# B's projection and split moved to the first stage, and one product with C per batch given to GpSimd

## The chip, the cores and the metric

One Trainium2 chip, one core, one launch. The metric is device time in microseconds. An execution of the kernel before takes 2493.12 us (median of three, 2491.65 to 2495.48). The engines are named as in the profile: PE is TensorE (PEld its weight loads), DVE is VectorE, ACT is ScalarE, POOL is GpSimd, SP is SyncE, which here only issues DMAs.

## What is computed

For 32 batches x of 512 rows and 256 columns, fp32: a layer norm without scale gives xn, and the output is the sum of x, a selective state-space scan and a mixture of experts that choose their rows.

```python
x, xn = x, layernorm(x)
# the scan, per batch: 256 channels d, 16 states s, 512 times l
deltaBC = xn @ W_deltaBC.T                    # 64 + 16 + 16 columns
delta, B, C = split(deltaBC, [64, 80])
delta = softplus(delta @ W_dt.T + b_dt)
h[l] = exp(delta[l] * A[s]) * h[l-1] + delta[l] * B[l, s] * xn[l]
y = sum_s h[l] * C[l, s] + D * xn
# the experts: 8 of them, each takes the 128 rows of a batch it likes best
S = softmax(xn @ Wg.T); G, I = top_k(S.T, 128)
out[I] += G * (gelu(xn[I] @ W1 + b1) @ W2 + b2)
return x + y + out
```

## The kernel before

Partitions hold channels in the scan (256 channels are two halves, so a tile of one batch is 128 partitions x 1024 columns, times along the columns) and rows elsewhere. The program is written out by hand, engine by engine, with semaphores; every engine runs its queue in order. There are three stretches.

**First stage** (`rows`, lines 285, 411, 539, 775 and 925; 32 iterations, software pipelined). SP loads x of batch b (line 293) into a ring of four and stores the normalized rows of batch b-3 to HBM (line 297). VectorE takes the statistics (801, 819, 828, 814), GpSimd the power and the last quarter of the normalization (417, 424), ScalarE the other three quarters (557). TensorE transposes xn (938), ScalarE copies the transposed tile to SBUF (567), and TensorE forms the router's logits (951) with weights widened so that four batches fill the 32 rows of one bank. Once per four batches VectorE copies these logits to SBUF (`lgt`, line 788), TensorE turns them to rows (960), and VectorE and ScalarE do the softmax. The load of batch b waits until batch b-4 is normalized.

**Top-k** (`top_round`, line 743): rounds of max, index, replace on VectorE for two halves of the batches. GpSimd gathers the chosen rows (`gather`, 447 to 449) once the first half's picks are out (855); TensorE transposes them (`chosen_columns`, 980).

**Main stage** (`main`, one iteration per batch and four slots `sl` of four steps each; step n of 16 is one state s). Per step:

- TensorE spreads row n of B over 128 partitions (`spread_b`, 1008), from `bcs`, which holds B as three bf16 parts whose sum is the fp32 value; it waits for the previous product with B, since there is one bank.
- VectorE runs the scan (896) over two banks `bank_x` that alternate, in place; then the product du x B of the next step (`multiply_b`, 842); then the product with C into one of four `prod` buffers (905).
- ScalarE makes the decays exp(delta A) (629), one slot ahead.
- GpSimd adds the product to `ysum` (494).

Between these, TensorE and ScalarE run the expert's two matrix products for a unit of 256 rows per slot (1102, 1121, 638, 688), GpSimd issues two gathers at the slot's first step (449) and two accumulating scatters at the second and third (513), and once per batch the accumulating store of y (526), which waits for y's own copies and, where a scatter to the same batch has just gone out, for its landing.

The next batch but one is prepared within a batch. `project` (966 to 972, at slot 0) computes the 96 rows of deltaBC; ScalarE copies them (`take_bc`, 580) and rounds them to bf16 (582); GpSimd subtracts (`take_rest`, 436, at slot 1); ScalarE rounds the rest (`take_mid`, 595); GpSimd subtracts again (`take_lo`, 442, at slot 2, after its step 9). SP moves C to HBM and the three parts of B to `bcs` (`move_high`, `move_mid`, `move_low`, 331 to 344), and loads C back, broadcast over the partitions, one slot ahead (`load_c`, 351). `expand` (977) multiplies by W_dt, ScalarE takes softplus (604 to 613), and GpSimd makes delta (457) and du = delta x xn (463) at slot 3, after its sum of step 12. `multiply_b` for step 0 of the next batch, issued by VectorE at step 15, waits for that du:

```python
dve.wait_ge(b_ready, s + 1)
dve.wait_ge(du_done, b + 1)
wait(dve, prod_done, s - 1)
```

Of the kernel before, what the change touches and what calls it, by code (L numbers as in the profile page):

```python
# [35 lines left out]
P = 128  # L36
# [4 lines left out]
BC = R + 2 * N  # L41
HALF = NB // 2
# [4 lines left out]
BODY = 4  # L47
BU = BODY * SLOTS
# [22 lines left out]
def build(nc, x, wdbc, wdt, bdt, alog, dpar, wg, w1, b1, w2, b2, out):  # L71
    ctx = ExitStack()
    with ctx:  # L73
# [10 lines left out]
        c_rows = nc.dram_tensor("c_rows", [NB, N, T], F32, kind="Internal").ap()  # L84
# [13 lines left out]
        wdbc_sb = sb("wdbc_sb", [P, HC, BC])  # L98
# [4 lines left out]
        wg_sb = sb("wg_sb", [P, HC, E])  # L103
# [14 lines left out]
        zabs = sb("zabs", [P, HC, T])  # L118
        yrow = sb("yrow", [P, TC, D])
        bc_all = sb("bc_all", [BC, T])  # L120
        bc_hi = sb("bc_hi", [P, T], BF16)
        bc_mid = sb("bc_mid", [P, T], BF16)
        bc_lo = sb("bc_lo", [P, T], BF16)
        bc_rest = sb("bc_rest", [P, T])
# [28 lines left out]
        wg_wide = small(HC * GATE, GATE * E)  # L153
        lgt = small(1, T)[0:GATE * E, 0]
        work = prod[:, 0, :, :]
        vals, idx_f = small(2, K), small(2, K)
# [22 lines left out]
        wide_set = sem("wide_set")  # L179
# [18 lines left out]
        lgt_done = sem("lgt_done")  # L198
# [17 lines left out]
        bc_proj = sem("bc_proj")  # L216
        hi_done = sem("hi_done")
        all_done = sem("all_done")
# [3 lines left out]
        hi_moved = sem("hi_moved")  # L222
        lo_moved = sem("lo_moved")
        mid_moved = sem("mid_moved")
# [8 lines left out]
        c_out = sem("c_out")  # L233
# [3 lines left out]
        prod_done = sem("prod_done")  # L237
        sum_done = sem("sum_done")
# [15 lines left out]
        def batch_of(u, i):  # L254

            return u // 64 * HALF + u % 8 * UB + i

# [13 lines left out]
        def _(sp):  # L271
# [12 lines left out]

            def rows(q):
                for r in range(ROWS):
# [22 lines left out]
            load_w2(0, 0, 0)  # L309

# [17 lines left out]
            def move_high(nb, par, used):  # L328

                held(all_done, nb)  # L330
                sp.dma_start(c_rows[nb - 1], bc_all[BC - N:BC, :]).then_inc(c_out, 16)
                held(hi_done, nb)
                held(b_ready, used)
                sp.dma_start(bcs[0:32, par], bc_hi[64:96, :]).then_inc(hi_moved, 16)

            def move_mid(nb, par):

                held(mid_done, nb)
                sp.dma_start(bcs[32:64, par], bc_mid[64:96, :]).then_inc(mid_moved, 16)

            def move_low(nb, par):

                held(lo_done, nb)
                sp.dma_start(bcs[64:96, par], bc_lo[64:96, :]).then_inc(lo_moved, 16)

            def load_c(u):

                held(c_out, (u // SLOTS + 1) * 16)
                held(prod_done, (u - 1) * STEPS)
                first = u % SLOTS * STEPS  # L350
                sp.dma_start(c_all[:, u % 2], c_rows[u // SLOTS:u // SLOTS + 1, first:first + STEPS, :]
                             .broadcast_to([P, STEPS, T])).then_inc(c_in[u % 2], 16)
# [44 lines left out]
        def _(pool):  # L397
# [33 lines left out]
            def take_rest(nb):  # L431

                pool.wait_ge(all_done, nb)
                pool.wait_ge(hi_done, nb)
                wait(pool, lo_done, nb - 1)
                nc.gpsimd.tensor_tensor(bc_rest[0:BC, :], bc_all[:], bc_hi[0:BC, :], ALU.subtract).then_inc(rest_done, 1)  # L436

            def take_lo(nb):

                pool.wait_ge(mid_done, nb)  # L440
                wait(pool, lo_moved, nb * 16 - 16)
                nc.gpsimd.tensor_tensor(bc_lo[0:BC, :], bc_rest[0:BC, :], bc_mid[0:BC, :], ALU.subtract).then_inc(lo_done, 1)

# [30 lines left out]
            def main(j):  # L474
                for k in range(BU):
# [56 lines left out]
        def _(act):  # L532
            for dst, src in ((wg_sb[:], wg.rearrange("(c p) e -> p c e", p=P)), (a_sb[:], alog), (b2_f, b2),
                             (wdbc_sb[:], wdbc.rearrange("(c p) m -> p c m", p=P)), (wdt_sb[:], wdt),
# [4 lines left out]
            def rows(q):  # L539
                for r in range(ROWS):  # L540
# [19 lines left out]
                    if there(b - 2, NB):  # L560
# [6 lines left out]
                        nc.scalar.copy(xtr[:, par], tr_banks[par]).then_inc(xnt_done, 2)  # L567
                    if r % GATE == 1 and there(g - 2, NB // GATE):
# [5 lines left out]
            def take_bc(nb):  # L574

                act.wait_ge(bc_proj, nb)
                wait(act, rest_done, nb - 1)
                wait(act, z_done, nb * 2 - 2)
                wait(act, c_out, nb * 16 - 16)
                nc.scalar.copy(bc_all[:], bank_t[0:BC, :]).then_inc(all_done, 1)  # L580
                wait(act, hi_moved, nb * 16 - 16)
                nc.scalar.copy(bc_hi[0:BC, :], bank_t[0:BC, :]).then_inc(hi_done, 1)  # L582
# [6 lines left out]

            def take_mid(nb):  # L590

                act.wait_ge(rest_done, nb)
                wait(act, mid_moved, nb * 16 - 16)
                wait(act, lo_done, nb - 1)
                nc.scalar.copy(bc_mid[0:BC, :], bc_rest[0:BC, :]).then_inc(mid_done, 1)

# [44 lines left out]
            def take_xr(b, par, dt):  # L641

                act.wait_ge(xr_tr, (b - 2) * HC + dt + 1)
                if dt == 0:
                    act.wait_ge(du_done, b - 1)
                    act.wait_ge(skip_done, b - 1)
                    act.wait_ge(bc_proj, b - 1)
# [15 lines left out]
            take_bc(1)  # L663
            take_mid(1)
# [5 lines left out]
            decays(0, 0, 0, 0, 1, range(STEPS))  # L670
            act.wait_ge(b1_in, 16)
# [3 lines left out]
            def main(j):  # L675
                for k in range(BU):
# [34 lines left out]
                    if there(b, NB) and there(b + 1, NB):  # L711
                        if sl == 2:
                            softplus_ln(b + 2)
                        if sl == 0:
                            take_bc(b + 2)
                        if sl == 1:
                            take_mid(b + 2)
# [455 lines left out]
```

## Time and profile before

| | |
|---|---|
| median of three runs | 2493.12 us |
| the profiled execution | 2495.35 us |
| its span | 2493.5 us |
| granted TensorE clock, mean | 0.982 |
| DMA | 325.4 MB, mean 130 GB/s |

The span is one execution from its first to its last instruction; the profiled execution's own time is 1.85 us longer. Busy times are sums over an engine's instructions, with overlaps counted once. A row of instructions reads: line, engine, operation, output<-input, shape, count | busy us, mean ns of one | idle time of the engine before them and what ended it. TensorE runs four passes over fp32 data, in two instructions. GpSimd's recorded durations include time spent behind an instruction that has not ended, so that start-to-start distances say more than means.

### The profile page before, as it was taken

The page shows a single profiled execution, that of the slowest core. Times are in us where ns is not written, and L with a number is a line of the kernel's source. Part 1 is how long each engine was busy: PE and PEld are TensorE (multiplying, and loading weights), DVE is VectorE, ACT ScalarE, POOL GpSimd, SP SyncE. Part 2 cuts the span into 40 slices and gives each one's busy share as a digit, 9 for nine tenths or more (in the row PEclk, how much of TensorE's full clock was granted, in tenths as well). Part 3 has the DMA queues.
Part 4 walks back from the last instruction along what each step waited for, and adds up shares of the span by engine and source line. Part 5 has one row for each costly group of instructions (what it writes and reads, how often), then busy time and mean ns, then how long its engine had stood idle before and what let it go on. Part 6 is the DMA issues. An engine that isn't in the chain of part 4 may idle for free. (4 is left out here: it accounts for less than half of the span.)

```text
span 2493.5 us, 32910 instructions
## 1 busy us (share of the span) xinstructions
PE 2356.9 (95%) x10524; PEld 1773.7 (71%) x10524; DVE 2417.3 (97%) x2090; ACT 1971.3 (79%) x3432; POOL 2200.3 (88%) x1260
## 2 busy tenths in 40 slices
PE   7828999999999999999999999999999999999996
PEld 3306777777777777777777777777777777777775
DVE  6599999999999999999999999999999999999995
ACT  6627888888888888888888888888888888888783
POOL 4316999999999999999999999999999999999996
PEclk9958999999999999999999999999999999999998
DMA  9872455444445453454535344444444445453443
GB/s 303 274 270 69 136 167 140 117 124 112 135 117 137 102 137 108 117 132 98 154 99 146 95 133 107 127 123 117 133 116 125 108 115 133 100 150 93 106 91 53
DMA packets 162973, 325.38 MB, mean 130 GB/s; under 512 B 16272, under 2 KB 133104, under 8 KB 146160
## 3 DMA queue, kind: packets, MB, share of 16 engines
q1 hardware_dynamic: 95536, 239.11, 28.0%
q0 software_dynamic: 66048, 83.92, 20.1%
q8 instruction: 85, 1.39, 0.2%
q14 instruction: 88, 0.72, 0.1%
q10 hardware_dynamic: 1216, 0.23, 0.0%
HBM read 250.84 MB, written 84.93 MB: 135 GB/s over the span
## 5 line engine op out<-in xcount | busy, mean ns | idle before, releaser
L494 POOL TENSOR_TENSOR ysum<-ysum,prod 128x1024 f32<-128x1024 f32 x480 | 1307.1, 2723 | 33.4 <-DVE prod L905 24.4
L896 DVE TENSOR_TENSOR_SCAN bank_x<-decay,bank_x 128x1024 f32<-128x1024 f32 x512 | 1167.2, 2280 | 0.0
L1102 PE MATMUL bank_l<-ext,w_sb 128*128 128x256 f32 x4096 | 970.3, 382 | 0.8 <-ACT og L688 0.8
L1121 PE MATMUL bank_l<-w_sb,hid 128*128 128x256 f32 x4096 | 957.2, 383 | 0.0
L1121 PEld LDWEIGHTS bank_l<-w_sb,hid 128*128 128x128 f32 x4096 | 762.6, 190 | 163.4 <-issue 67.7
L1102 PEld LDWEIGHTS bank_l<-ext,w_sb 128*128 128x128 f32 x4096 | 756.5, 190 | 136.2 <-issue 23.5
L638 ACT ACTIVATE hid<-bank_l,b_all 128x256 f32<-128x256 f32 x1024 | 430.9, 475 | 332.6 <-PE bank_l L1102 329.4
L629 ACT ACTIVATE decay<-delta,a_sb 128x511 f32<-128x511 f32 x1024 | 640.0, 708 | 1.2
L905 DVE TENSOR_TENSOR prod<-bank_x,c_all 128x1024 f32<-128x1024 f32 x512 | 620.4, 1212 | 0.1
L842 DVE TENSOR_TENSOR bank_x<-du,bank_b 128x1024 f32<-128x1024 f32 x512 | 613.4, 1198 | 0.0
L513 POOL DMA_INDIRECT out<-og,idx_all x256 | 408.6, 1596 | 49.5 <-POOL ysum L494 35.4
L449 POOL DMA_INDIRECT ex<-xn_rows,idx_all x256 | 258.0, 1008 | 85.2 <-issue 47.0
L1008 PE MATMUL bank_b<-bcs,pick 96*128 96x512 bf16 x512 | 197.4, 386 | 35.4 <-DVE bank_x L842 28.8
L1008 PEld LDWEIGHTS bank_b<-bcs,pick 96*128 96x128 bf16 x512 | 49.5, 97 | 147.3 <-DVE bank_x L842 118.6
L629 ACT ACT_TABLE_LOAD x98 | 125.7, 1283 | 4.2 <-POOL delta L457 2.5
L722 ACT ACT_TABLE_LOAD x95 | 121.9, 1283 | 1.7
L688 ACT ACTIVATE og<-bank_l,gate_all 128x256 f32<-128x256 f32 x256 | 105.0, 460 | 11.3 <-PE bank_l L1121 11.3
L494 POOL TENSOR_TENSOR ysum<-skip,prod 128x1024 f32<-128x1024 f32 x32 | 91.8, 2868 | 11.1 <-DVE prod L905 11.1
L654 ACT COPY ext<-bank_t 128x512 f32<-128x512 f32 x128 | 76.0, 594 | 28.0 <-PE bank_t L986 28.0
L417 POOL TENSOR_TENSOR hid<-hid,neg_half 128x4 f32<-128x4 f32 x32 | 32.3, 1008 | 68.0 <-DVE hid L828 65.9
L436 POOL TENSOR_TENSOR bc_rest<-bc_all,bc_hi 96x512 f32<-96x512 f32 x32 | 68.7, 2146 | 19.9 <-ACT bc_hi L582 19.9
L986 PE MATMUL bank_t<-ident,ex 128*128 128x128 f32 x512 | 77.3, 274 | 6.6 <-DMA ex<-xn_rows,idx_all 6.6
(95 smaller groups left out, 1577.9 us busy)
## 6 DMA issues: line engine op xcount, KB each, us to landing
c_all<-c_rows SPq DMA_DIRECT2D x128, 1024.0 KB, 5.4
w_sb<-in_w SPq DMA_DIRECT2D x32, 1024.0 KB, 6.2
decay<-in_x SPq DMA_DIRECT2D x32, 512.0 KB, 5.4
xn_rows<-decay SPq DMA_DIRECT2D x32, 512.0 KB, 4.0
out<-yrow POOLq DMA_DIRECT2D x32, 512.0 KB
xr<-xn_rows SPq DMA_DIRECT2D x30, 512.0 KB, 6.5
ex<-xn_rows,idx_all POOLq DMA_INDIRECT x256
out<-og,idx_all POOLq DMA_INDIRECT x256, 4.1
```

The source lines that it names most:

```text
L449: pool.indirect_dma_start(out=ex[:, u % 2, i], out_offset=None, in_=xn_rows, in_offset=bass.IndirectOffsetOnAxis(ap=idx_all[:, u * UB + i: ...
L494: nc.gpsimd.tensor_tensor(ysum[:, m % 2], first, prod[:, i], ALU.add).then_inc(sum_done, 1)
L513: pool.indirect_dma_start(out=out_rows, out_offset=bass.IndirectOffsetOnAxis(ap=idx_all[:, w * UB + c:w * UB + c + 1], axis=0), in_=og[:, ...
L629: nc.scalar.activation(decay[:, par, i, dt, 1:T], delta[:, dpar_, dt, 1:T], ACT.Exp, scale=a_sb[:, dt, n:n + 1]).then_inc(decay_done, 1)
L638: nc.scalar.activation(hid[:, k % 2, f], bank_l[(pair + k) % 2][:, (f % 2) * UT:(f % 2 + 1) * UT], ACT.Gelu_apprx_tanh, bias=b1_all[:, exp ...
L722: nc.scalar.activation(warm[:], bdt_sb[:, 0:1], ACT.Gelu_apprx_tanh)
L842: nc.vector.tensor_tensor(bank_x[:, s % 2].rearrange("p (c t) -> p c t", c=HC), du[:, par], bank_b[:][:, None, :].broadcast_to([P, HC, T]) ...
L896: nc.vector.tensor_tensor_scan(bank_x[:, s % 2], decay[:, k % 2, i].rearrange("p c t -> p (c t)"), bank_x[:, s % 2], 0.0, ALU.mult, ALU.ad ...
L905: nc.vector.tensor_tensor(prod[:, i], bank_x[:, s % 2].rearrange("p (c t) -> p c t", c=HC), c_all[:, u % 2, i][:, None, :].broadcast_to([P ...
L1008: nc.tensor.matmul(bank_b[:], pick[:, n:n + 1].broadcast_to([3 * 2 * N, P]), bcs[:, par], start=True, stop=True).then_inc(b_ready, 1)
L1102: i = nc.tensor.matmul(bank_l[(q + k) % 2][:, (f % 2) * UT:(f % 2 + 1) * UT], w1_sb[:, e2, hc, f * P:(f + 1) * P], ext[:, k % 2, hc], star ...
L1121: i = nc.tensor.matmul(o, hid[:, (k - 1) % 2, f, c * K:(c + 1) * K], w2_sb[:, le2, f], start=False, stop=(f == FC - 1 and c == UB - 1))
```

## The change

B and C are projected in the first stage: the router's weights and those of deltaBC stand side by side (`wpj_sb`, 8 + 96 columns), each batch's 104 rows are copied by ScalarE into a ring of four (`proj`), and SP stores 96 of them to HBM (`bc_rows`) and the 16 rows of B to SBUF, eight batches to a tile of 128 partitions (`b_whole`). The split of B into three bf16 parts is then done on four such tiles, between the first stage and the main stage, and stored to HBM (`b_rows`). In the main stage SP loads the 64 rows for `expand` (`load_rank`, slot 0) and the three parts of B (`load_b`, slot 1) per batch. `project`, `take_bc`, `take_rest`, `take_mid`, `take_lo` and the `move_` functions are gone; so are the widened weights and VectorE's copy of the logits.

Step n = 4 of each batch: the scan writes to a tile in SBUF (`state`), VectorE leaves out the product with C, and GpSimd does it, ahead of its sum.

```diff
+PJ = E + BC
+SPLIT = P // N
+NG = NB // SPLIT
+GP_STEP = 4
...
+        def gp_prods(s):
+
+            return (s + N - 1 - GP_STEP) // N
+
+        def dve_prods(s):
+
+            return s - gp_prods(s)
...
+            def store_proj(b):
+
+                held(proj_done, b + 1)
+                sp.dma_start(bc_rows[b], proj[E:PJ, b % 4]).then_inc(proj_out[b % 4], 16)
+                sp.dma_start(b_whole[b % SPLIT * N:b % SPLIT * N + N, b // SPLIT],
+                             proj[E + R:E + R + N, b % 4]).then_inc(proj_out[b % 4], 16)
+
+            def store_parts(g):
+
+                for part, done in enumerate((hi_done, mid_done, lo_done)):
+                    held(done, g + 1)
+                    sp.dma_start(b_rows[part, g * P:(g + 1) * P, :], b_parts[:, part, g % 2]).then_inc(parts_out[g % 2], 16)
+
+            def load_b(nb, par, used):
+
+                g = (nb - 1) // SPLIT
+                held(parts_out[g % 2], (g // 2 + 1) * 48)
+                held(b_ready, used)
+                held(stack_set, 1)
+                for part in range(3):
+                    sp.dma_start(bcs[2 * N * part:2 * N * part + N, par],
+                                 b_rows[part, nb * N - N:nb * N, :]).then_inc(b_in[par], 16)
+
+            def load_rank(nb):
+
+                held(z_done, nb * 2 - 2)
+                sp.dma_start(rank[:], bc_rows[nb - 1, 0:R, :]).then_inc(rank_in, 16)
...
+                    if there(b - 6, NB):
+                        store_proj(b - 6)
...
             load_w2(0, 0, 0)
+            for r in range(4):
+                held(proj_out[r], 32 * NB // 4)
+            load_rank(1)
+            store_parts(0)
+            load_b(1, 0, 0)
...
-            move_high(1, 0, 0)
-            move_mid(1, 0)
-            move_low(1, 0)
             load_c(0)
+            for g in range(1, NG):
+                store_parts(g)
             for part in range(4, HALF // UB):
                 residual(part)
...
+                    if sl == 0 and there(b + 1, NB):
+                        load_rank(b + 2)
                     if sl == 1 and there(b + 1, NB):
-                        move_high(b + 2, (m + 1) % 2, b * N)
-                    if sl == 2 and there(b + 1, NB):
-                        move_mid(b + 2, (m + 1) % 2)
-                    if sl == 3 and there(b + 1, NB):
-                        move_low(b + 2, (m + 1) % 2)
+                        load_b(b + 2, (m + 1) % 2, b * N)
...
         @block.gpsimd
-            take_rest(1)
-            take_lo(1)
+            split_rest(0)
+            split_lo(0)
             take_delta(1, 0)
             take_du(1, 0, 16)
+            for g in range(1, NG):
+                split_rest(g)
+                split_lo(g)
...
-                            pool.wait_ge(prod_done, s + 1)
+                            if n == GP_STEP:
+                                pool.wait_ge(scan_done, s + 1)
+                                pool.wait_ge(c_in[u % 2], (u // 2 + 1) * 16)
+                                wait(pool, sum_done, s - 3)
+                                nc.gpsimd.tensor_tensor(prod[:, i], state[:], c_all[:, u % 2, i][:, None, :].broadcast_to([P, HC, T]),
+                                                        ALU.mult).then_inc(gp_prod_done, 1)
+                                pool.wait_ge(gp_prod_done, b + 1)
+                            else:
+                                pool.wait_ge(prod_done, dve_prods(s + 1))
...
-                        if sl == 1 and i == 0 and there(b, NB) and there(b + 1, NB):
-                            take_rest(b + 2)
-                        if sl == 2 and i == 1 and there(b, NB) and there(b + 1, NB):
-                            take_lo(b + 2)
...
         @block.scalar
+                    if there(b - 3, NB):
+                        act.wait_ge(logits_done, b - 2)
+                        wait(act, proj_out[(r - 3) % 4], (b - 3) // 4 * 32)
+                        wait(act, lg_tr, (b - 3) // GATE)
+                        nc.scalar.copy(proj[:, (r - 3) % 4], lg_banks[(r - 3) % 2][0:PJ, :]).then_inc(proj_done, 1)
...
             skip_term(0, 16, 0)
-            take_bc(1)
-            take_mid(1)
+            split_hi(0)
+            split_mid(0)
...
             decays(0, 0, 0, 0, 1, range(STEPS))
+            for g in range(1, NG):
+                split_hi(g)
+                split_mid(g)
...
         @block.vector
-                    if r % GATE == 3 and there(g - 1, NB // GATE):
-
-                        dve.wait_ge(logits_done, g * GATE)
-                        wait(dve, lg_tr, g - 1)
-                        nc.vector.tensor_copy(lgt, lg_banks[gp][0:GATE * E, :]).then_inc(lgt_done, 1)
...
-                wait(dve, prod_done, s - 1)
+                if (s - 2) % N == GP_STEP:
+                    wait(dve, scan_done, s - 1)
+                else:
+                    wait(dve, prod_done, dve_prods(s - 1))
...
-                        nc.vector.tensor_tensor_scan(bank_x[:, s % 2], decay[:, k % 2, i].rearrange("p c t -> p (c t)"),
+                        if n == GP_STEP:
+                            wait(dve, gp_prod_done, b)
+                            into = state[:].rearrange("p c t -> p (c t)")
+                        else:
+                            into = bank_x[:, s % 2]
+                        nc.vector.tensor_tensor_scan(into, decay[:, k % 2, i].rearrange("p c t -> p (c t)"),
                                                      bank_x[:, s % 2], 0.0, ALU.mult, ALU.add).then_inc(scan_done, 1)
...
+                        if n == GP_STEP:
+                            continue
...
         @block.tensor
                         for hc in range(HC):
-                            i = nc.tensor.matmul(lg[0:GATE * E, :], wg_wide[:, hc * GATE + place], xtr[:, pp, hc],
-                                                 start=(place == 0 and hc == 0), stop=(place == GATE - 1 and hc == HC - 1))
+                            i = nc.tensor.matmul(lg_banks[pp][0:PJ, :], wpj_sb[:, hc], xtr[:, pp, hc],
+                                                 start=(hc == 0), stop=(hc == HC - 1))
...
-                        pe.wait_ge(lgt_done, g)
+                        pe.wait_ge(proj_done, g * GATE)
                         wait(pe, lsh_done, g - 1)
                         for c in range(TC):
-                            i = nc.tensor.transpose(bank_t[:, c * GATE * E:(c + 1) * GATE * E], lgt[:, c * P:(c + 1) * P],
-                                                    ident[0:GATE * E, 0:GATE * E])
+                            for place in range(GATE):
+                                i = nc.tensor.transpose(bank_t[:, (c * GATE + place) * E:(c * GATE + place + 1) * E],
+                                                        proj[0:E, place, c * P:(c + 1) * P], ident[0:E, 0:E])
...
-                pe.wait_ge(all_done, nb)
-                nc.tensor.matmul(bank_t[:], wdt_sb[:, dt * P:(dt + 1) * P], bc_all[0:R, :],
+                pe.wait_ge(rank_in, nb * 16)
+                nc.tensor.matmul(bank_t[:], wdt_sb[:, dt * P:(dt + 1) * P], rank[:],
```

## Rows read from the trace of the kernel before

**Rows 1.** The page, part 1: busy us of each engine, share of the span, instructions.

```profile
PE 2356.9 (95%) x10524; PEld 1773.7 (71%) x10524; DVE 2417.3 (97%) x2090; ACT 1971.3 (79%) x3432; POOL 2200.3 (88%) x1260
```

**Rows 2.** Busy us by stretch: PE, PEld, DVE, ACT, POOL, then granted clock, DMA share, GB/s.

```profile
50.00:70.00 20.00, 17.97 (x78) 7.60 (x76) 13.91 (x71) 14.36 (x26) 8.48 (x13) 1.00 0.99 328
...
90.00:122.00 32.00, 26.48 (x106) 11.49 (x107) 17.69 (x87) 20.31 (x36) 11.79 (x16) 0.89 0.67 218
...
192.00:2480.00 2288.00, 2245.31 (x10085) 1725.52 (x10084) 2273.30 (x1538) 1870.42 (x3268) 2134.02 (x1174) 1.00 0.46 119
```

**Rows 3.** Timeline of VectorE from 1112 us: start, duration, engine, line.

```profile
1112.16 2.28 DVE L896 TENSOR_TENSOR_SCAN bank_x<-decay,bank_x 128x1024 f32<-128x1024 f32 x1
1114.35 1.20 DVE L842 TENSOR_TENSOR bank_x<-du,bank_b 128x1024 f32<-128x1024 f32 x1
1115.47 1.21 DVE L905 TENSOR_TENSOR prod<-bank_x,c_all 128x1024 f32<-128x1024 f32 x1
1116.60 2.28 DVE L896 TENSOR_TENSOR_SCAN bank_x<-decay,bank_x 128x1024 f32<-128x1024 f32 x1
```

**Rows 4.** Line 494, 780 to 1350 us: durations min/median/max ns, first and last start.

```profile
L494 POOL TENSOR_TENSOR ysum<-skip,prod x8: 2867/2878/2887, 840.7 to 1336.6; 128x1024 f32<-128x1024 f32 x8
```

**Rows 5.** Groups of GpSimd: the sums, 780 to 1350 us, then the whole span.

```profile
L494 POOL TENSOR_TENSOR ysum<-ysum,prod 128x1024 f32<-128x1024 f32 x122 | 334.4, 2741 | 2.8
...
L494 POOL TENSOR_TENSOR ysum<-ysum,prod 128x1024 f32<-128x1024 f32 x480 | 1307.1, 2723 | 33.4 <-DVE prod L905 24.4
```

**Rows 6.** Timeline of GpSimd: in the top-k, then from 1106 and from 1147 us.

```profile
140.63 1.15 POOL L436 TENSOR_TENSOR bc_rest<-bc_all,bc_hi 96x512 f32<-96x512 f32 x1 [19.90 <-ACT bc_hi L582]
...
1106.60 2.35 POOL L457 TENSOR_TENSOR delta<-delta,zabs 128x1024 f32<-128x1024 f32 x1
1109.08 2.37 POOL L463 TENSOR_TENSOR du<-delta,xnt 128x1024 f32<-128x1024 f32 x1
...
1147.46 2.38 POOL L494 TENSOR_TENSOR ysum<-ysum,prod 128x1024 f32<-128x1024 f32 x1
1150.01 1.64 POOL L513 DMA_INDIRECT out<-og,idx_all  x1 [0.17 <-POOL ysum L494]
...
1163.14 2.38 POOL L494 TENSOR_TENSOR ysum<-ysum,prod 128x1024 f32<-128x1024 f32 x1
...
1166.80 1.62 POOL L513 DMA_INDIRECT out<-og,idx_all  x1 [0.17 <-issue]
```

**Rows 7.** Timeline of GpSimd at 715 us, batch 7: the store of y.

```profile
715.09 1.39 POOL L526 DMA_DIRECT2D out<-yrow  x1 [2.05 <-DMA out<-og,idx_all]
```

**Rows 8.** Who waited for whom, 780 to 1350 us: total us, times, longest.

```profile
PEld bank_b L1008 <- DVE bank_x L842: 28.2, 63, 0.6
```

**Rows 9.** Groups of VectorE, ScalarE and TensorE, 0 to 137 us.

```profile
L801 DVE BATCH_NORM_STATS2 hid<-decay 128x6 f32<-128x256 f32 x128 | 44.7, 409 | 26.8 <-DMA decay<-in_x 26.8
...
L788 DVE COPY hid<-bank_x 32x512 f32<-32x512 f32 x8 | 5.4, 679 | 16.1 <-PE bank_x L951 16.1
...
L557 ACT ACTIVATE decay<-decay,hid 128x256 f32<-128x256 f32 x96 | 50.6, 591 | 31.1 <-DVE hid L814 31.0
...
L960 PE MATMUL bank_t<-ident,hid 32*128 32x32 f32 x32 | 3.4, 227 | 0.8 <-DVE hid L788 0.8
```

**Rows 10.** DMA queues, 0 to 115 us: packets, MB, share of 16 engines.

```profile
q1 hardware_dynamic: 33019, 34.34, 90.5%
```

**Rows 11.** Timeline of the hand-over, 154 to 192 us, and DMA issues 125 to 192 us.

```profile
154.26 5.00 ACT L629 ACTIVATE decay<-delta,a_sb 128x511 f32<-128x511 f32 x8
...
181.61 1.24 POOL L449 DMA_INDIRECT ex<-xn_rows,idx_all  x1 [26.30 <-DVE gate_all L855]
...
186.03 1.09 PE L986 MATMUL bank_t<-ident,ex 128*128 128x128 f32 x4 [6.64 <-DMA ex<-xn_rows,idx_all]
...
191.76 0.47 PE L1033 MATMUL bank_l<-ident,hid 128*128 128x128 f32 x1 [4.64 <-DVE hid L848]
...
out<-in_x SPq DMA_DIRECT2D x10, 11.8
```

More of the change, by code:

```diff
@@ L118, in build @@
         zabs = sb("zabs", [P, HC, T])
+        state = sb("state", [P, HC, T])
         yrow = sb("yrow", [P, TC, D])
[L120 to L124, printed above, removed]
+        rank = sb("rank", [R, T])
+        b_parts = sb("b_parts", [P, 3, 2, T], BF16)
         bcs = sb("bcs", [3 * 2 * N, 2, T], BF16)
@@ L152, in build @@
         lmax, lsum, lrec = (small(2, TC * GATE) for _ in range(3))
-        wg_wide = small(HC * GATE, GATE * E)
-        lgt = small(1, T)[0:GATE * E, 0]
         work = prod[:, 0, :, :]
+        proj = prod[0:PJ, 2:4, :, :].rearrange("p a b t -> p (a b) t")
+        b_whole = ysum[:, :, :, :].rearrange("p a b t -> p (a b) t")
         vals, idx_f = small(2, K), small(2, K)
@@ L197, in build @@
         logits_done = sem("logits_done")
-        lgt_done = sem("lgt_done")
+        proj_done = sem("proj_done")
+        proj_out = [sem(f"proj_out{i}") for i in range(4)]
         lg_tr = sem("lg_tr")
@@ L221, in build @@
         lo_done = sem("lo_done")
-        hi_moved = sem("hi_moved")
-        lo_moved = sem("lo_moved")
-        mid_moved = sem("mid_moved")
+        parts_out = [sem(f"parts_out{i}") for i in range(2)]
+        rank_in = sem("rank_in")
+        b_in = [sem(f"b_in{i}") for i in range(2)]
         z_done = sem("z_done")
@@ L326, in _ @@
                 residual(part)
[L328 to L344, printed above, removed]
             def load_c(u):
-                held(c_out, (u // SLOTS + 1) * 16)
-                held(prod_done, (u - 1) * STEPS)
+                held(prod_done, dve_prods((u - 1) * STEPS))
+                held(gp_prod_done, gp_prods((u - 1) * STEPS))
                 first = u % SLOTS * STEPS
-                sp.dma_start(c_all[:, u % 2], c_rows[u // SLOTS:u // SLOTS + 1, first:first + STEPS, :]
+                sp.dma_start(c_all[:, u % 2], bc_rows[u // SLOTS:u // SLOTS + 1, R + N + first:R + N + first + STEPS, :]
                              .broadcast_to([P, STEPS, T])).then_inc(c_in[u % 2], 16)
-            move_high(1, 0, 0)
-            move_mid(1, 0)
-            move_low(1, 0)
             load_c(0)
+            for g in range(1, NG):
+                store_parts(g)
             for part in range(4, HALF // UB):
@@ L429, in _, with split_rest, split_lo @@
                 pool.wait_ge(rows_out[r], 16 * NB // 4)
[L431 to L442, printed above, removed]
+            def split_rest(g):
+                pool.wait_ge(hi_done, g + 1)
+                nc.gpsimd.tensor_tensor(b_whole[:, g], b_whole[:, g], b_parts[:, 0, g % 2], ALU.subtract).then_inc(rest_done, 1)
+            def split_lo(g):
+                pool.wait_ge(mid_done, g + 1)
+                wait(pool, parts_out[g % 2], g // 2 * 48)
+                nc.gpsimd.tensor_tensor(b_parts[:, 2, g % 2], b_whole[:, g], b_parts[:, 1, g % 2], ALU.subtract).then_inc(lo_done, 1)
             def gather(u):
@@ L572, in _, with split_hi, split_mid @@
             through(rows, NB // ROWS)
[L574 to L582, printed above, removed]
+            def split_hi(g):
+                for r in range(4):
+                    act.wait_ge(proj_out[r], (g + 1) * SPLIT // 4 * 32)
+                wait(act, parts_out[g % 2], g // 2 * 48)
+                nc.scalar.copy(b_parts[:, 0, g % 2], b_whole[:, g]).then_inc(hi_done, 1)
+            def split_mid(g):
+                act.wait_ge(rest_done, g + 1)
+                wait(act, parts_out[g % 2], g // 2 * 48)
+                nc.scalar.copy(b_parts[:, 1, g % 2], b_whole[:, g]).then_inc(mid_done, 1)
             def take_yrow(half, taken, added):
@@ L588, in take_yrow @@
                 nc.scalar.copy(yrow[:, 2 * half:2 * half + 2], bank_t[:].rearrange("p (c d) -> p c d", c=2)).then_inc(yrow_done, 1)
[L590 to L595, printed above, removed]
             def take_z(nb, par, dt):
@@ L768, in parameters @@
                 nc.vector.tensor_copy(b2_lo, b2_f).then_inc(b2_step, 1)
-                for hc in range(HC):
-                    for place in range(GATE):
-                        dve.wait_ge(wide_set, 1)
-                        nc.vector.tensor_copy(wg_wide[:, hc * GATE + place, place * E:(place + 1) * E], wg_sb[:, hc]).then_inc(wide_set, 1)
             def rows(q):
@@ L1009, in spread_b, with stack_whole @@
                                  start=True, stop=True).then_inc(b_ready, 1)
-            def stack_whole(b):
-                pe.wait_ge(hi_moved, b * 16 + 16)
-                pe.wait_ge(mid_moved, b * 16 + 16)
-                pe.wait_ge(lo_moved, b * 16 + 16)
+            def stack_whole(par, count):
+                pe.wait_ge(b_in[par], count)
             pe.wait_ge(pick_made, 4)
@@ L1036, in _ @@
             picks_lines(0)
-            stack_whole(0)
+            stack_whole(0, 48)
             spread_b(0, 0, 0)
@@ L1072, in main @@
                                 pe.wait_ge(xnt_in[m % 2], (b // 2 + 1) * 16 + (sl + 1) * 16 // HC)
-                            if sl == 1 and there(b + 1, NB):
-                                pe.wait_ge(all_done, b + 2)
-                                pe.wait_ge(hi_done, b + 2)
                             if sl == 2 and there(b + 1, NB):
```

45 lines of the change are left out of this document (12 added, 33 removed).

## The prediction

> **What bounds it now.** I read the busy totals first, then the stages, then a step of VectorE, then GpSimd. VectorE is busy 2417 us and GpSimd 2200, TensorE 2357 [rows 1]. By stage [rows 2], the first stage (layernorm, router, rows written) runs to about 122 us with the DMA engines at a share of 0.99 until 90 and 0.67 after that; the top-k rounds fill the time to 192; the main stage lasts 2288 us, of which VectorE works 2273. There one step is scan, next product with B, product with C, starting at 1112.16, 1114.35, 1115.47, and the next scan at 1116.60 [rows 3]: 2.19 + 1.12 + 1.13 = 4.44 us, so 71.04 us for a batch of sixteen. VectorE never pauses.
>
> GpSimd is the one to look at twice. Its share, 88%, suggests room. But eight starts of its first sum of a batch lie between 840.7 and 1336.6 us, seven intervals of **70.84 us**, 0.20 less than VectorE's 71.04 [rows 4]. In the same stretch its 122 other sums waited 2.8 us in all [rows 5]. What the page counts as idle there is gaps between instructions, not waiting. Its lag shrinks by 0.2 us per batch and that is all the slack it has; over the whole run its sums waited 24.4 us for VectorE's product [rows 5], most of it in the first two and the last batch, where its DMAs are fewer.
>
> Where does GpSimd hold VectorE? Not at the sums: four buffers of products let it lag three steps, 13 us. At du: the product with B for step 0 of the next batch is issued behind the scan of step 15 and waits for du, which GpSimd makes only after sum 12. Du starts at 1109.08 and takes 2.37, so it is there at 1111.45; the product starts at 1114.35 [rows 3, 6]. Slack: **2.9 us**.
>
> **The change, part by part.**
>
> VectorE in the main stage: one product with C per batch goes. The step keeps 2.19, and the next scan now directly follows the product with B whose output it needs, so that one shows its full 1.20 and not 1.12, with a few hundredths for the semaphore. 4.44 becomes about 3.43: 1.0 us per batch, 32 us in all, if nothing else holds it. The scan that writes to SBUF I take at the old 2.19: it reads the same operands, one in SBUF and one in PSUM. Bounds: it may be a few hundredths shorter or longer, 32 x 0.1 = 3 us each way.
>
> GpSimd in the main stage: bc_rest and bc_lo go, the multiply comes. Rest takes 1.15 us where nothing overlaps it, at 140.63 [rows 6]; the 2.1 us mean of the page counts time behind an earlier instruction. Lo: from the sum at 1163.14 to the scatter at 1166.80 is 3.66, the same pair without lo is 1147.46 to 1150.01, 2.55, so 1.11. Removed: 2.26. The multiply has the shape of delta and du (128x1024 f32): delta to du, start to start, is 2.48 [rows 6], and the sum behind the multiply waits for it like du for delta. Added: 2.3 to 2.5; I take 2.45. Net +0.19, so GpSimd's own batch is 70.84 + 0.19 = 71.03 us, against a VectorE that could do 70.0. **The product leaves one full engine for another full one.** From the third or fourth batch on VectorE, 2.9 us ahead, stalls about 1 us per batch at the product with B for step 0, and the period stays 71.0.
>
> Bounds of the multiply: at 2.3 the net is +0.04, 29 batches give 4 us less; at the mean that the page's rows give for a sum, 2.72 [rows 5], plus 0.15 for the dependence, +0.6, 12 us more. I take 2.45 because the nearest row is du's. GPSIMD Engine Reference of the Trainium skill, section 3.1, gives 4497 ns for an fp32 tensor_tensor of 2048 columns, half of which is 2.25 us here, an estimate; by it the main stage would come out 6 us shorter than by the 2.45 taken.
>
> What GpSimd's timeline gives: in the first two batches it waits for VectorE, and so wins about 1.5 us there from the shorter step. At batch 7, and by the same condition at 23, it waits 2.05 us at the output DMA of y for its own scatter to land [rows 7]; 0.2 of that is an ordinary gap. Before, VectorE did not feel it (the lag ate it); now GpSimd sets the pace and both count: 2 x 1.85 = 3.7. Twenty-nine batches at 71.03 for 71.04: -0.3. GpSimd at the last du: +1.9. VectorE may be 2.9 ahead of where it stood: -1.0; its last batch has no du behind it and gives its own -1.0. **Main stage: -2 us**, from -9 to +12.
>
> TensorE: the projection leaves the main stage (4 passes of 512 columns, under 2 us per batch) and sixteen spreads of B stay. Its weight load waited 28.2 us for VectorE's product with B in 128 steps [rows 8], 0.22 per step; so it has 3.5 us per batch before and about 5 after. One short step of 3.4 us leaves it behind by less than 1 us, and the spread is early by more. Nothing. ScalarE loses three copies per batch; it waits for TensorE anyway: nothing. SP's queue in the main stage: four small moves go, four come (rank, three of B) ahead of load_rows; the loads of C keep their place. Nothing: they are needed several steps later.
>
> First stage. The matmul has 104 output rows for 32, same columns: no cost. ScalarE gets a copy of about 0.6 us per batch; it idled 31.1 us for VectorE's shift over 32 batches [rows 9], so most is covered. Sixteen transposes of 8 rows per group for four: 3.4 us of TensorE for 32 now [rows 9], about 10 us for 128, spread over 32 batches, covered except once at the end (+1.3 us). VectorE's copy of the logits goes and with it 16.1 us of in-order waiting for TensorE [rows 9], which delayed the statistics behind it.
>
> The DMAs are what counts. Each batch stores 96 rows of 2 KB to HBM and 16 rows to SBUF: 229 KB beside 1049 KB. The engines moved 34.3 MB in 33019 packets with 90.5% of their time [rows 10] (115 us): 50 ns per 1 KB packet, and 328 GB/s at share 0.99 [rows 2]. So a batch was 3.2 us and the stores add 0.70. Twenty-six batches are stored before the last load. Those of the first 90 us, some 21, cost in full, for the engines are full there: 15 us. The others fall where a third of DMA time is idle [rows 2], and there VectorE's waits for the logits go too: I give back 6. **First stage: +9, with its end +10**, from +2 (the stores fill gaps, the stall was the limit) to +24 (0.70 plus some of SP's two further issues, on each of 26 batches, and nothing given back).
>
> The hand-over. VectorE's top-k follows the first stage without a gap, so the chain of batch 0 (skip, split, z, softplus, delta, du, decays) is hidden: its decays ended at 159.3 while VectorE left its rounds at 191.7 [rows 11]. It starts ahead by no projection and now has split 0 in it; same length. But SP is now held in the stores of splits 1 to 3, which ScalarE makes only behind the first decays, some 34 us into the top-k; six residual parts (11.8 us each to landing in their queue [rows 11]) and two weight loads go out behind them and meet the first gather. That one was issued at 181.61 and consumed at 186.03, and the second TensorE step needed by VectorE came at 191.76; 4.6 us of room [rows 11]. I take **+2**, from 0 to +8.
>
> Sum: +10 + 2 - 2 = +10 us. The profiled execution took 2495.35 us, its span 2493.5, so 2505.4; the median of the three runs is 2.2 lower: **2503 us**.
>
> **Rivals.**
>
> *The saving arrives.* GpSimd's own batch falls to 70.0 or the idle 5% of its share is real. VectorE then saves 32 us: 2493 - 32 + 12 = 2473. It decides if the multiply costs under 1.5 us. For it: the share in the totals. Against: [rows 4, 6]. Chance 0.08.
>
> *The first stage hides its stores.* It was bound by the loop load, statistics, normalize, next load, with VectorE's wait for the logits in it. Then +2, hand-over 0 and main -6: 2489. For it: VectorE waited 26.8 us for loads and 16.1 for logits [rows 9], so both limits are near. Against: share 0.99. Chance 0.17.
>
> *Small DMAs cost by the piece.* Two more per batch on one queue, each with an issue of its own; if 0.9 us of issue adds to the 0.70: 26 x 1.6 = +42, 2533. For it: the load is issued behind them. Against: the issues run while the engines still work on the last store. Chance 0.07. DMA: Bandwidth & Descriptors of the Trainium skill, section on measured bandwidth, says that transfers under 64 KB are dominated by descriptors; the 16-row store is 32 KB.
>
> *GpSimd's multiply is dear* (2.9 to 3.0 with its waits): VectorE follows at 71.5, main +12, 2517. Chance 0.10.
>
> **How the numbers follow.** Forecast 0.58 at 2503, its own range 2494 to 2513. A change of 0.2%, 5 us, is about what a measurement can tell. Faster (below 2488): the first rival and part of the second, 0.15. Same (2488 to 2498): the rest of the second and the low side of the forecast, 0.22. Slower: 0.63. For 8 in 10 the range is 2486 to 2518.
>
> **What would show it.** Right: GpSimd's first sums 71.0 us apart; VectorE idle ahead of the product with B about 1 us per batch, released by du; the short step 3.4 us; the multiply 2.3 to 2.5 us; first stage share near 1 to its end, top-k starting about 10 us later. Wrong: VectorE without idle time in the main stage, first sums 70.0 apart, or a first stage that ends at 137 as before.

## The result: 2506.06 us, 0.45% slower

The median of six runs is 2506.06 us (2501.0 to 2509.6), beside 2493.19 for the kernel before (six runs): a ratio over the runs of 1.0045, 95% interval 1.0033 to 1.0056. The medians differ by 12.9 us (a quotient of 1.0052, inside the interval); 2503 was forecast. The profiled execution, the slowest of the six, spans 2507.8 us, 14.3 more than before, and this difference can be placed. The page of the kernel after, part 1, answers to [rows 1]; the stretches (PE, PEld, DVE, ACT, POOL, granted clock, DMA share, GB/s) to [rows 2]:

```profile
PE 2301.7 (92%) x10492; PEld 1770.6 (71%) x10492; DVE 2383.0 (95%) x2042; ACT 1949.0 (78%) x3376; POOL 2217.3 (88%) x1236
```
```profile
50.00:70.00 20.00, 16.27 (x77) 9.44 (x76) 10.72 (x57) 14.78 (x27) 7.76 (x11) 0.91 1.02 328
...
90.00:122.00 32.00, 23.84 (x120) 14.38 (x119) 15.11 (x79) 20.29 (x36) 10.76 (x15) 0.89 0.99 327
...
205.00:2490.00 2285.00, 2185.43 (x9961) 1704.86 (x9961) 2242.74 (x1505) 1830.48 (x3176) 2142.97 (x1143) 1.00 0.46 120
```

VectorE's total fell by 34 us and nothing came of it: in the main stage it is now busy 2243 of 2285 us. The DMA engines, at 0.67 of their time from 90 to 122 us before, are at 0.99 there.

**First stage and hand-over.** VectorE's timeline after; the statistics of the last batch began at 116.45 before, VectorE's first product with B at 191.62, its first scan 1.55 later:

```profile
127.67 1.41 DVE L818 BATCH_NORM_STATS2 hid<-decay 128x6 f32<-128x256 f32 x4 [2.60 <-DMA decay<-in_x]
...
202.71 1.22 DVE L862 TENSOR_TENSOR bank_x<-du,bank_b 128x1024 f32<-128x1024 f32 x1
207.56 0.37 DVE L875 CAST idx_all<-bank_l 128x128 uint32<-128x128 f32 x1 [3.62 <-PE bank_l L1047]
...
208.00 2.27 DVE L921 TENSOR_TENSOR_SCAN bank_x<-decay,bank_x 128x1024 f32<-128x1024 f32 x1
```

The first stage gives +11.1 (202.71 against 191.62) and the hand-over +3.7 (from the product to the scan 5.29 against 1.55 us). In the second, VectorE waited for TensorE, and TensorE for the gathered rows:

```profile
206.01 1.09 PE L1003 MATMUL bank_t<-ident,ex 128*128 128x128 f32 x4 [15.52 <-DMA ex<-xn_rows,idx_all]
```

**Main stage.** From the first scan to the end of the last product, 2271.9 us after (208.00 to 2479.90) and 2272.2 before. VectorE's timeline at a batch's end and at its step 4:

```profile
1122.48 2.29 DVE L921 TENSOR_TENSOR_SCAN bank_x<-decay,bank_x 128x1024 f32<-128x1024 f32 x1
1125.67 1.23 DVE L862 TENSOR_TENSOR bank_x<-du,bank_b 128x1024 f32<-128x1024 f32 x1 [0.90 <-POOL du L484]
...
1145.70 2.28 DVE L921 TENSOR_TENSOR_SCAN state<-decay,bank_x 128x1024 f32<-128x1024 f32 x1
1147.89 1.21 DVE L862 TENSOR_TENSOR bank_x<-du,bank_b 128x1024 f32<-128x1024 f32 x1
1149.23 2.30 DVE L921 TENSOR_TENSOR_SCAN bank_x<-decay,bank_x 128x1024 f32<-128x1024 f32 x1
```

The short step is 3.53 us for 4.44 [rows 3]: 0.91 gained. At the end of the same batch VectorE waits 0.90 for du. Over the run that wait is the largest that VectorE has in the main stage (groups of VectorE, whole span):

```profile
L862 DVE TENSOR_TENSOR bank_x<-du,bank_b 128x1024 f32<-128x1024 f32 x512 | 617.1, 1205 | 24.9 <-POOL du L484 24.9
L921 DVE TENSOR_TENSOR_SCAN state<-decay,bank_x 128x1024 f32<-128x1024 f32 x32 | 72.9, 2277 | 0.0
```

GpSimd, its timeline around the same places and its first sums (800 to 1370 us), which answer to [rows 4, 6]:

```profile
1123.21 2.37 POOL L484 TENSOR_TENSOR du<-delta,xnt 128x1024 f32<-128x1024 f32 x1
...
1153.64 1.95 POOL L554 DMA_DIRECT2D out<-yrow  x1
1154.50 3.51 POOL L514 TENSOR_TENSOR prod<-state,c_all 128x1024 f32<-128x1024 f32 x1
1158.08 2.36 POOL L526 TENSOR_TENSOR ysum<-ysum,prod 128x1024 f32<-128x1024 f32 x1
```
```profile
L526 POOL TENSOR_TENSOR ysum<-skip,prod x8: 2892/2898/2922, 853.5 to 1352.4; 128x1024 f32<-128x1024 f32 x8
```

Seven intervals in 498.9 us: 71.27 us per batch in the mean, where it was 70.84. Six of them are 71.13 to 71.20 us; the seventh, from 1209.25 to 1281.24, is 71.99 and has in it a wait of 0.76 us at the store of y. So GpSimd's ordinary batch is 71.17 us. Du ends at 1125.58 and VectorE's product starts 0.09 later. The page's 3407 ns mean for the multiply counts the tail of the DMA issue ahead of it; from that issue's end, 1155.59, to the multiply's, 1158.01, are 2.42 us.

### The profile page after: what moved, and what is told of

The parts are those of the page before. It is cut to its first block and busy times, and to the rows that moved or that the text cites. A ratio compares the mean times of both kernels' runs of the same rounds, so it can differ in the third digit from the quotient of the medians.

```text
span 2507.8 us, 32574 instructions
## 1 busy us (share of the span) xinstructions
PE 2301.7 (92%) x10492; PEld 1770.6 (71%) x10492; DVE 2383.0 (95%) x2042; ACT 1949.0 (78%) x3376; POOL 2217.3 (88%) x1236
## 5 line engine op out<-in xcount | busy, mean ns | idle before, releaser
L526 POOL TENSOR_TENSOR ysum<-ysum,prod 128x1024 f32<-128x1024 f32 x480 | 1274.3, 2655 | 25.8 <-DVE prod L932 12.5
L921 DVE TENSOR_TENSOR_SCAN bank_x<-decay,bank_x 128x1024 f32<-128x1024 f32 x480 | 1097.5, 2286 | 4.6 <-DVE bank_x L862 0.5
L862 DVE TENSOR_TENSOR bank_x<-du,bank_b 128x1024 f32<-128x1024 f32 x512 | 617.1, 1205 | 24.9 <-POOL du L484 24.9
L932 DVE TENSOR_TENSOR prod<-bank_x,c_all 128x1024 f32<-128x1024 f32 x480 | 584.6, 1218 | 0.1
L749 ACT ACT_TABLE_LOAD x95 | 121.9, 1283 | 1.7
L514 POOL TENSOR_TENSOR prod<-state,c_all 128x1024 f32<-128x1024 f32 x32 | 109.0, 3407 | 0.0
L818 DVE BATCH_NORM_STATS2 hid<-decay 128x6 f32<-128x256 f32 x128 | 44.9, 413 | 55.8 <-DMA decay<-in_x 55.8
```

The costliest lines, as they stand in the source:

```text
L526: nc.gpsimd.tensor_tensor(ysum[:, m % 2], first, prod[:, i], ALU.add).then_inc(sum_done, 1)
L749: nc.scalar.activation(warm[:], bdt_sb[:, 0:1], ACT.Gelu_apprx_tanh)
L862: nc.vector.tensor_tensor(bank_x[:, s % 2].rearrange("p (c t) -> p c t", c=HC), du[:, par], bank_b[:][:, None, :].broadcast_to([P, HC, T]) ...
L921: nc.vector.tensor_tensor_scan(into, decay[:, k % 2, i].rearrange("p c t -> p (c t)"), bank_x[:, s % 2], 0.0, ALU.mult, ALU.add).then_inc( ...
L932: nc.vector.tensor_tensor(prod[:, i], bank_x[:, s % 2].rearrange("p (c t) -> p c t", c=HC), c_all[:, u % 2, i][:, None, :].broadcast_to([P ...
```

## The experiments

Each experiment was timed beside runs of the kernel before, whose median was 2494.34 or 2494.69 us (2493.19 beside the change). Ratios are to those runs; the times are medians, and a difference of two experiments' medians carries about 1.5 us from this.

**e1: the product back to VectorE.**

```diff
         def gp_prods(s):
 
-            return (s + N - 1 - GP_STEP) // N
+            return sum(1 for b in range(NB) if gp_batch(b) and b * N + GP_STEP < s)
+
+        def gp_batch(b):
+
+            return False
...
-                            if n == GP_STEP:
+                            if n == GP_STEP and gp_batch(b):
```

> The changed kernel with the product of step 4 given back to VectorE in every batch; projection and split stay in the first stage. If GpSimd sets the pace of the main stage (its batch 71.17 us, of which the multiply is some 2.5): GpSimd falls to about 68.7 us per batch, VectorE never waits for du and runs at 71.03, and the main stage is as long as with the product on GpSimd: 2506 us, within 3. If instead GpSimd's product does save VectorE its 0.91 us in most batches: 32 x 0.9 = 29 us more, 2535.

2508.74 us, ratio 1.0057 (1.0041 to 1.0072), which overlaps the change's. From the first scan to the end of the last product it takes 2272.3 us, for 2271.9 with the product on GpSimd. VectorE's wait for du is gone and its batch is 71.03 us. Moving a whole product per batch off the engine that was 97% busy was worth nothing in the main stage; so the 12.9 us are not the product's either.

**e2: no multiply.**

```diff
                                 pool.wait_ge(scan_done, s + 1)
-                                pool.wait_ge(c_in[u % 2], (u // 2 + 1) * 16)
-                                wait(pool, sum_done, s - 3)
-                                nc.gpsimd.tensor_tensor(prod[:, i], state[:], c_all[:, u % 2, i][:, None, :].broadcast_to([P, HC, T]),
-                                                        ALU.mult).then_inc(gp_prod_done, 1)
-                                pool.wait_ge(gp_prod_done, b + 1)
```

(and the two waits for `gp_prod_done` on SP and VectorE)

> The changed kernel without GpSimd's multiply (the product of state 4 with C is left out of the output; the sum adds what lies in its buffer, so the sums stay sixteen). If the multiply's time on GpSimd is what VectorE waits for at du: no wait there, batches of 70.12 us, 32 x 0.9 = 29 us less, 2477. If the wait at du has another origin (ScalarE's softplus late, the scatters, TensorE): GpSimd's batch shrinks but the wait stays, 2500 to 2506.

2479.06 us, ratio 0.9941 (0.9926 to 0.9956): 27 us less than the change; its output lacks the product of step 4. From the first scan to the end of the last product it takes 2244.7 us, 27.2 less. The wait for du is gone (groups of VectorE, whole span):

```profile
L856 DVE TENSOR_TENSOR bank_x<-du,bank_b 128x1024 f32<-128x1024 f32 x512 | 616.5, 1204 | 0.6 <-PE bank_b L1018 0.6
```

So the saving of 0.91 us per batch is real and is kept back by the multiply's time on GpSimd, by nothing on ScalarE or TensorE.

**e3: two batches of three.** As e1, with `return b % 3 != 2`.

> The product of step 4 is GpSimd's in two batches of three, VectorE's in the third. If both engines' loads simply add: GpSimd 3 x 71.17 - 2.5 = 211.0 us for three batches, VectorE 3 x 71.03 - 2 x 0.91 = 211.3, so both near 70.4 per batch and the slack of 2.9 us at du carries the difference: 32 x 0.6 = 19 us less, 2487. If GpSimd's bound is not its own load but something that scales with every batch: 2500 or more.

2487.89 us, ratio 0.9972 (0.9962 to 0.9982): faster than the kernel before, with every result computed. The two engines' loads do add as supposed: GpSimd's first sums in eight batches, and VectorE's product with B:

```profile
L530 POOL TENSOR_TENSOR ysum<-skip,prod x8: 2878/2893/2911, 849.5 to 1342.9; 128x1024 f32<-128x1024 f32 x8
```
```profile
L866 DVE TENSOR_TENSOR bank_x<-du,bank_b 128x1024 f32<-128x1024 f32 x512 | 617.7, 1206 | 0.6 <-POOL du L488 0.6
```

70.49 us per batch, and 0.6 us of waiting for du in the whole run. Each engine has a little left in the average; the slack at du carries the two heavy batches.

**e7: the product alone, in the kernel before.** The edits of step 4 and their counts put into the kernel before; projection and split stay where they were.

> The kernel before with GpSimd's product alone; projection and split stay in the main stage. If GpSimd paces: its batch is 70.85 + 0.32 + 2.26 = 73.4 us, 2.4 above VectorE's 71.03, over 30 batches +72, with the waits at y that now show (+3.7) less VectorE's head start of 3 and its last batch: 2565. If GpSimd has the room that its share of 88% suggests: VectorE's saving arrives, 32 x 0.9 = 29 us less, 2464.

2558.16 us, ratio 1.0255 (1.0240 to 1.0271). The first sums lie (1367.1 - 853.5) / 7 = 73.37 us apart, as forecast; VectorE waits for du in nearly every batch:

```profile
L514 POOL TENSOR_TENSOR ysum<-skip,prod x8: 2890/2904/2913, 853.5 to 1367.1; 128x1024 f32<-128x1024 f32 x8
```
```profile
L865 DVE TENSOR_TENSOR bank_x<-du,bank_b 128x1024 f32<-128x1024 f32 x512 | 616.7, 1204 | 88.6 <-POOL du L475 88.6
```

The total was put 7 us too high. Counted from the first scan, GpSimd's last first sum comes 67.6 us later than before, where 72 + 3.7 had been forecast. The waits at the store of y are a part of that: the longer intervals around them (73.58 to 73.81) add some 1.4 us in all for the 3.7. The rest is that about 29 batches, not 30, ran 2.3 us longer, not 2.4. This run also gives both terms of GpSimd's sum by themselves. Six of the seven intervals above are 73.29 to 73.36 us, 73.34 in the mean. So the product costs 73.34 - 70.84 = **2.50 us** per batch, and taking the split out of the main stage gives 73.34 - 71.17 = **2.17**.

**e5 and e6: what the first stage pays for.**

```diff
                 sp.dma_start(bc_rows[b], proj[E:PJ, b % 4]).then_inc(proj_out[b % 4], 16)
+                sp.dma_start(bc_twice[b], proj[E:PJ, b % 4]).then_inc(proj_out[b % 4], 16)
```

> In the changed kernel each batch's 96 projected rows are stored to HBM twice, the second time to a tensor that nobody reads: 197 KB more per batch. If the first stage is bound by bytes on the DMA engines: 0.60 us at 328 GB/s on 26 batches, +16, 2522. If it is bound by the piece (issue and completion of each DMA): 0.9 us or more each, +23 or more, 2530. If it is bound by ScalarE's copies or the loop of load and normalization: under +6, 2506 to 2512.

```diff
-                sp.dma_start(b_whole[b % SPLIT * N:b % SPLIT * N + N, b // SPLIT],
-                             proj[E + R:E + R + N, b % 4]).then_inc(proj_out[b % 4], 16)
...
             load_rank(1)
+            for g in range(NG):
+                sp.dma_start(b_whole[:, g], bc_rows[g * SPLIT:(g + 1) * SPLIT, R:R + N, :]).then_inc(whole_in[g], 16)
             store_parts(0)
```

> The changed kernel without the 16-row store to SBUF per batch: the tiles of B for the split are loaded from HBM in four DMAs after the first stage. One DMA of 32 KB less per batch. By bytes: 0.10 us on 26 batches, -2.6, 2503.5. By the piece: 0.4 us or more each, -10 or more, 2496 or less. If the loads afterwards delay the chain of batch 0 they are hidden behind the top-k.

e5: 2524.57 us, 1.0121 (1.0105 to 1.0136), 18.5 more than the change, where 16 were due by bytes and 23 or more by the piece. Its last batch's statistics start at 141.37 us, 14.8 later than the mean of the kernels with the change's first stage, which is 0.57 us for a store of 197 KB. So bytes bind, and not ScalarE's copies or the load loop.

e6: 2499.53 us, 1.0022 (1.0013 to 1.0031), 6.5 less than the change and between my two figures. In e6's timeline of VectorE the last batch's statistics start at 121.53, where the change's start at 127.67:

```profile
121.53 1.40 DVE L818 BATCH_NORM_STATS2 hid<-decay 128x6 f32<-128x256 f32 x4 [1.95 <-DMA decay<-in_x]
```

One execution of each is not enough here. The six kernels whose first stage is the change's (after, e1 to e4, e9) start these statistics between 123.6 and 128.4 us, 126.6 in the mean; the three without the small store (e6, e8, e10) between 119.7 and 121.9, 121.1 in the mean. That is 5.5 us on 26 batches, or 0.21 for a store of 32 KB whose bytes are worth 0.10. The medians say less. E6's 6.5 us hold a shorter hand-over too: its first scan is 1.56 us behind the product and not 5.29. E8, which has e6's edit and e3's with a hand-over as long as e3's (5.43 and 5.34 us), is 4.2 us faster than e3, or 0.16 per store, with intervals that overlap. DMA: Bandwidth & Descriptors of the Trainium skill, section on measured bandwidth, calls transfers below 64 KB descriptor-dominated. A price above that of the bytes goes that way, but between 0.10 and 0.21 us these runs do not settle it. Why e6's hand-over is short is open: SP's order behind the split is the change's, and in e8, which has the same loads of B, the wait is back.

**e4 and e9: the hand-over.** e4 puts `residual(4..7)` ahead of `store_parts(1..3)`. e9 adds:

```diff
-                    if sl != 0:
+                    if sl != (1 if b == 0 else 0):
                         continue
```

> SP issues the four residual parts before the stores of splits 1 to 3 and not after them. If the first gather lay behind the residual copies on the DMA engines: they are done before it is issued, TensorE takes it about 2 us after its issue, VectorE's wait of 3.6 us between its first product with B and its first scan goes, 2502. If it lay behind the two residual parts and two weight loads of the first batch, which stay behind the splits: 2504 to 2506, the wait stays over 2 us.

> The changed kernel with four residual parts ahead of the split stores, as in e4, and the first batch's two residual parts and two weight loads one slot later, behind the start of the main stage. If these loads are what held the first gather in e4 (its wait stayed at 4.0 us): from VectorE's first product with B to its first scan 1.56 us as in the kernel before, not 5.3 or 4.0, and 3.7 us less than the change: 2502. If the gather is slow for another reason (the index table, the loads of C): the wait stays near 4, 2504 to 2506.

e4: 2504.26 us, 1.0041 (1.0027 to 1.0054); from the product with B to the first scan it takes 4.04 us. That is no gain that the runs can show: in four other kernels whose SP still has the change's order (e1, e2, e3 and e5) this wait is 4.01, 4.44, 5.34 and 4.69 us. So the other bulk has to be in the gather's way: the first batch's two residual parts and two weight loads. e9: 2502.98 us, 1.0037 (1.0023 to 1.0050), and in its timeline of VectorE the scan is 1.55 us behind the product again:

```profile
198.92 1.22 DVE L862 TENSOR_TENSOR bank_x<-du,bank_b 128x1024 f32<-128x1024 f32 x1
...
200.47 2.28 DVE L921 TENSOR_TENSOR_SCAN bank_x<-decay,bank_x 128x1024 f32<-128x1024 f32 x1
```

The gather itself shows it more clearly. From the start of its first issue on GpSimd to TensorE's first transpose of its rows are 4.4 us before, 12.0 to 13.4 in after, e1, e2, e3 and e5, 12.1 in e4 and 12.0 in e8, but 6.6 in e9 and 7.5 in e10. The medians fall by 1.8 us (e4) and 3.1 (e9), with intervals that overlap the change's; that the first batch's loads held the gather is shown by the timelines, its worth in the total only to within these.

**e8 and e10: together.** e8 is e3, e4 and e6 in one; e10 adds the edit of e9.

> Two of three batches on GpSimd, residual parts ahead of the split stores, and B loaded after the first stage, together. If the three are independent: 2506 - 19 - 3.7 - 2.6 = 2481, below the kernel before (2493). If the first stage hands its delay over to GpSimd or the gather (they compete for the same head start): 2485 to 2490.

> As e8 (two of three batches, residual parts first, B loaded later), with the first batch's bulk loads one slot later too. If the wait of e8 at the first scan (5.4 us) was theirs: 1.56 us there and 3.9 less than e8, 2480. If it was the slower split chain: as e8, 2484.

e8: 2483.71 us, 0.9960 (0.9946 to 0.9974); its first scan comes 5.43 us behind the product. e10: **2480.59 us, 0.9946 (0.9932 to 0.9959)**, 14 us below the kernel before of the same group, and that wait is 2.18 us, not 1.56. This beats both kernels. The gains measured for e3, e4 and e6 by themselves (18.2, 1.8 and 6.5 us) add up to 2479.6, so e8 is 4.1 us short. That is about the size of e6's shorter hand-over, which e8 does not have. The share that comes from the last edit is inside the intervals.

The second rival for that wait, the slower split chain, has a part too. With the residual parts ahead, ScalarE's first copy of the last split waits 15.3 us for the split stores that landed late, where it waited 3.46 in the change. So GpSimd comes to the gather late, 7.4 us ahead of VectorE's first product, not 10.0. ScalarE's timeline in e10:

```profile
184.35 0.62 ACT L616 CAST b_parts<-ysum 128x512 bf16<-128x512 f32 x1 [15.30 <-DMA b_rows<-b_parts]
```

## Why the prediction was right

The time, 2503 against 2506.06, and its sign came from three terms, +10, +2 and -2. The profiled execution has +11.1, +3.7 and -0.3. It is the slowest of its six. Over the profiled executions of the six kernels with the change's first stage (two with the stage of before) the first product with B comes 10.0 us later in the mean, and over the five with the change's order of SP the wait behind it is 3.2 us longer. With -0.3 for the main stage that is 12.9 us, the difference of the medians.

*Main stage: -2 forecast, -0.3 measured.* The step it rested on, that GpSimd's own batch (70.84 us) and not its share of 88% is its load, holds in all four kernels that vary it: GpSimd's product removed (e2), given back (e1), thinned (e3) and put where the split still stood (e7). The place where VectorE feels it, du at step 15, is where 24.9 us of waiting now stand. Two terms were a little off. The multiply was put at 2.45 us, with its wait, and is 2.50 (e7); the split was put at 2.26 removed and is 2.17. Together GpSimd's ordinary batch is 71.17 us, not 71.03, which is 4 us over 29 batches. A third term was off the other way: the waits at the store of y, put at 2 x 1.85 = 3.7 us. The two intervals between first sums in which they lie are 71.58 and 71.62, so 0.4 each, and a third, the 71.99 above, adds 0.8: 1.7 in all. The scatters landed sooner: in batch 7 the store of y starts 4.3 us after the scatter, where it was 6.0 before; why is open. So the misses of +4 and -2 us half cancel, which was luck. VectorE's short step saves 0.91 us, not 1.0: the scan that follows its own input directly starts 1.34 us after the product, not 1.24. Its head start was spent as forecast. GPSIMD Engine Reference of the Trainium skill, section 3.1, would have had the multiply at 2.25 us, an estimate from half of its 2048 columns; the row of du was nearer.

*First stage with its end: +10 forecast, +11.1 measured.* The forecast was 15 for the stores of the first 90 us, 6 given back behind them, and 1 for the end. The statistics of batch 26, with 20 or 21 batches stored ahead of them, start at 92.16 us before and at 106.15 after: +14.0, or 0.67 to 0.70 per batch. From there to the last batch's statistics it took 24.3 us before and 21.5 after: -2.8, not -6. From those to the first product with B nothing is added (-0.1), where 1 was forecast. So the price by bytes held, which e5 and the share of 0.99 bear out, and the late idle time did take the last stores in and gave something back, but half of what was put down. Over the six executions the two parts are +13.2 and -2.0, since the first stage repeats to a few us only.

*Hand-over: +2 forecast, +3.7 measured.* The mechanism, SP held in the split stores and its bulk loads meeting the first gather, is what e9 removes. Of the bulk that the prediction named, the first batch's residual parts and weight loads are what e9 shows to matter; a share of the four residual parts ahead of them is not shown (e4). What was too small was the size: the room of 4.6 us was used up and 2.5 to 3.8 more, not 2.

The rivals: the saving did not arrive (e1, e7), the first stage did not hide its stores, small DMAs cost by the piece at most a quarter of what that rival asked, and the multiply was not dear (2.50 us for 2.9 to 3.0). No experiment tried the first stage without ScalarE's copy or without TensorE's extra transposes, so what of the 11.1 us is theirs stays open; e5 says only that bytes bind. TensorE's granted clock from 50 to 70 us was 0.91 after and 1.00 before; what that costs there was not tested either.

## What to carry to other kernels

Before moving work off the busiest engine, measure the other engine's own period: the distance between like instructions in a stretch where it waits for nobody, and not its busy share. Then find the one place where the first waits for the second, and what slack it has. Where two engines are both within a per cent of full, moving the work in every period can gain nothing, as here, while moving it in some of the periods (here two of three) splits the gain between them.

## What the runs showed of the hardware

A scan into SBUF costs VectorE what one into PSUM does: 2277 against 2286 ns. GpSimd's instructions beside one such scan keep their distances: sum, scatter and sum start at 1143.54, 1146.07 and 1147.14 us, 2.53 and 1.07 apart, and a slot earlier, beside scans into PSUM, 2.53 and 1.08. SBUF — State Buffer of the Trainium skill, in its section on who interferes with whom, says that an instruction of VectorE with at most one SBUF input, outside the two-port modes, doesn't contend with GpSimd; the scan has one SBUF input in either form, and these rows agree.

What I had not expected is how much the first stage wanders. With one and the same first stage, the last batch's statistics began anywhere from 123.6 to 128.4 us in six profiled executions, while the main stage of this kernel took 2270.8 to 2273.2 us in five (after, e4, e5, e6 and e9).
